# First mixture of experts by routed token rows instead of all experts over all tokens

## What is computed

```python
x = ln(x + L0_attn(x))    # 16 heads of 8, each token sees 7 neighbours
x = ln(x + L0_xattn(x))   # additive attention over 77 context tokens, tanh, two gates
x = ln(x + L0_ffn(x))     # first mixture, below
x = ln(x + L1_attn(x))    # keeps the 32 largest scores of each token
x = ln(x + L1_xattn(x))   # softmax attention over the context
x = ln(x + L1_ffn(x))     # second mixture: 8 experts (GELU, 256 hidden), one shared

def L0_ffn(x):            # 8 experts, 512 hidden, the best 2 of each token count
    probs = softmax(x @ gate_w.T); w, idx = top_k(probs, 2); w = w / w.sum()
    combine = zeros(T, 8).at[arange(T), idx].add(w)
    for gup, dn, ce in experts:
        g, u = split(x @ gup.T, 2)
        acc = acc + ce[:, None] * (silu(g) * u @ dn.T)
```

## Time and profile before

| | |
|---|---|
| Median of 2 runs | 874.55 us (874.15 to 874.95) |
| The profiled execution | 871.73 us, of it 869.9 us span |
| TensorE busy, share of the span | 736.0 us, 85% |
| VectorE, ScalarE, GpSimd busy | 505.5, 410.6, 77.0 us |
| Mean granted TensorE clock | 0.934 of full speed |
| First mixture's stage, batches 0 to 3 | 97.2, 96.8, 97.2, 76.1 us |

### The profile page before, as it was taken

The page is one execution under the profiler, slowest core; times in us unless marked ns, Lnnn a source line. Parts: engine busy times, 40 slices in busy tenths (PEclk is TensorE's granted clock), DMA queues, the critical chain, the costliest instruction groups (busy, mean ns, idle before and its releaser), DMA issues.

```text
span 869.9 us, 10866 instructions
## 1 busy us (share of the span) xinstructions
PE 736.0 (85%) x4056; PEld 511.7 (59%) x4056; DVE 505.5 (58%) x1420; ACT 410.6 (47%) x652; POOL 77.0 (9%) x71
## 2 busy tenths in 40 slices
PE   3468679999987999999978999999978999963596
PEld 1211157876244976775345967865347888843486
DVE  3678455654765675643845675733946754448344
ACT  1058643237875453247874443166964522211142
POOL 2100020100011120100011120100011000000100
PEclk8769879999999999999999999999999999986588
DMA  7025000000000010000000010000000000000000
GB/s 244 0 73 205 1 28 1 1 1 2 1 3 0 1 41 1 1 1 1 1 3 0 2 41 0 1 2 1 1 3 1 1 13 1 1 0 1 0 1 13
DMA packets 6549, 15.02 MB, mean 17 GB/s; under 512 B 2776, under 2 KB 2912, under 8 KB 6240
## 3 DMA queue, kind: packets, MB, share of 16 engines
q1 hardware_dynamic: 6496, 14.32, 4.9%
HBM read 13.27 MB, written 1.05 MB: 16 GB/s over the span
## 4 chain that ended last, share of the span: by engine, by line
PE 59%; DVE 17%; ACT 15%; issue 7%; POOL 1%; DMA 1%; SPq 1%; POOLq 0%; DVEq 0%; ACTq 0%
PE bank L642 12%; ACT a_big L846 9%; PE bank L503 7%; PE bank L504 7%; PE bank L505 7%; PE bank L760 6%; PE bank L601 6%; PE bank L695 2%; PE bank L675 2%; PE bank L517 1%; DVE a_big L1032 1%; DVE a_big L1377 1%; PE bank L552 1%; DVE top L1260 1%; DVE b_big L1264 1%
## 5 line engine op out<-in xcount | busy, mean ns | idle before, releaser
L877 ACT ACTIVATE b_big<-bank 128x512 f32<-128x512 f32 x128 | 75.2, 596 | 174.0 <-PE bank L505 173.8
L1228 DVE TENSOR_TENSOR b_big<-bank,b_big 128x512 f32<-128x512 f32 x128 | 87.8, 689 | 117.2 <-PE bank L505 66.8
L846 ACT ACTIVATE a_big<-a_sum,txt_cols 128x512 f32<-128x512 f32 x231 | 145.6, 715 | 14.2 <-PE bank L601 14.1
L601 PE MATMUL bank<-a_big,score_pad 128*32 128x512 f32 x616 | 143.9, 615 | 7.4 <-ACT a_big L966 5.8
L642 PEld LDWEIGHTS bank<-down_sb,b_big 128*128 128x128 f32 x1024 | 118.6, 192 | 6.5 <-issue 4.2
L642 PE MATMUL bank<-down_sb,b_big 128*128 128x128 f32 x1024 | 119.8, 275 | 0.5 <-DVE b_y L1217 0.5
L503 PE MATMUL bank<-x_hi,gup_hi 128*128 128x512 f32 x256 | 110.3, 431 | 5.2 <-ACT b_big L877 3.1
L504 PE MATMUL bank<-x_hi,gup_lo 128*128 128x512 f32 x256 | 101.8, 398 | 0.0
L505 PE MATMUL bank<-x_lo,gup_hi 128*128 128x512 f32 x256 | 101.8, 397 | 0.0
L601 PEld LDWEIGHTS bank<-a_big,score_pad 128*32 128x32 f32 x616 | 28.3, 109 | 101.3 <-ACT a_big L846 54.7
L760 PEld LDWEIGHTS bank<-rw_sb,b_big 128*128 128x128 f32 x576 | 71.6, 196 | 3.1
(11 more groups left out here) (216 smaller groups left out, 940.8 us busy)
## 6 DMA issues: line engine op xcount, KB each, us to landing
b_big<-gup SPq DMA_DIRECT2D x8, 512.0 KB, 7.1
down_sb<-down SPq DMA_DIRECT2D x1, 2048.0 KB, 8.5
rw_sb<-rw SPq DMA_DIRECT2D x1, 1152.0 KB, 10.8
a_T<-x_T SPq DMA_DIRECT2D x4, 256.0 KB, 2.5
a_tok<-x_tok SPq DMA_DIRECT2D x4, 256.0 KB, 2.9
b_big<-rw SPq DMA_DIRECT2D x2, 512.0 KB, 3.5
y<-b_tok SPq DMA_DIRECT2D x4, 256.0 KB, 2.0
const_sb<-const SPq DMA_DIRECT2D x1, 872.0 KB
```

The source lines that it names most:

```text
L601: last = mm(P[2][32 * j:32 * j + 32, :], score_pad[:, 31 - i:63 - i], ring[k % RING], start=(i == 0), stop=(KCOL * (i + 1) + j >= KEYS))
L846: act(ring[k % RING], a_sum[:, 0:S], ACT.Tanh, bias=txt_cols[:, c:c + 1])\
L877: act(th[n % 3], P[3 + 2 * (c % 2)][:, :], ACT.Silu).then_inc(th_ready, 1)
L1228: tt(hid[e % 2][:, c * S:(c + 1) * S], P[4 + 2 * (c % 2)][:, :], th[n % 3], ALU.mult)\
```

## The change

Only `swiglu` of every batch and what feeds it change. The tokens are no longer run through all experts. For each token the two best experts are found by rank (`rank_x2`, nine DVE instructions). `positions` on PE sums one-hot rows over earlier tokens, and `place_x2` (ten DVE instructions) turns that into a slot for each of the 1024 pairs of token and expert, sorted by expert, every expert beginning at a multiple of 128. That needs at most NT = 15 tiles of 128 rows. `scatter` on POOL writes the rows of x2 to their slots in device memory with 8 indirect DMAs of 128 rows of 512 bytes; `load_rows` on SP reads them back with 4 DMAs. For each tile PE loads the expert's offset into a register, transposes 128 rows, forms gate and up part in two halves of 256 hidden units with the tokens as stationary and the weights as moving operand (512 columns), transposes the product back in 4 pieces and does 4 down matmuls, whose weights are chosen by the register. The results go to device memory by 15 DMAs (`store_rows`), `gather` on POOL reads them back to token order with 8 indirect DMAs, and 8 DVE instructions weigh and add them. There are 30 steps of half a tile instead of 32; the steps of `attend_nearby` keep their numbers. A cleared x_rows and a separate load of the table `expand` come into the start of the program.

```diff
+NT = 2 * S // 128 + E - 1
+X_GROUPS = ((0, 1), (1, 3), (3, 7), (7, NT))
...
-SCORE_AT = (25, 28, 29, 31)
+SCORE_AT = (26, 28, 29)
...
+            def load_rows(b):
+                eng.wait_ge(scattered, 2 * T * 16 * (b + 1))
+                if b == 0:
+                    eng.wait_ge(split_done, len(raw))
+                else:
+                    eng.wait_ge(xout_psum, b)
+                for g, (i, z) in enumerate(X_GROUPS):
+                    eng.dma_start(rows_in[:, i * 128:z * 128].rearrange("p (i f) -> p i f", f=128),
+                                  x_rows[i * 128:z * 128, :].rearrange("(i p) f -> p i f", p=128))\
+                        .then_inc(rows_loaded[g], 16)
...
+            def store_rows(b):
+                if b >= 1:
+                    for t in range(T):
+                        eng.wait_ge(picked_in[t], 32 * b)
+                for i in range(NT):
+                    eng.wait_ge(y_ready, NT * b + i + 1)
+                    eng.dma_start(y_rows[i * 128:(i + 1) * 128, :], rows_out[i % 4]).then_inc(y_stored[i % 4], 16)
...
+            def positions(b):
+                eng.wait_ge(top_ready, b + 1)
+                at = P[2][:, 64:64 + (T + 1) * E]
+                mm(at, const_of("earlier"), r_top[:, :], start=True, stop=False)
+                for t in range(T):
+                    last = mm(at[:, (t + 1) * E:].rearrange("p (t e) -> p t e", e=E), ones[:, :],
+                              r_top[:, t * E:(t + 1) * E].unsqueeze(1).broadcast_to([128, T - t, E]),
+                              start=False, stop=(t == T - 1))
+                last.then_inc(pos_psum, 1)
...
+                def expert(i):
+                    at[i] = eng.value_load(offsets[0:1, i:i + 1], min_val=0, max_val=(E - 1) * I0)
...
+                def turn_x(i):
+                    for g, (first, end) in enumerate(X_GROUPS):
+                        if i == first:
+                            eng.wait_ge(rows_loaded[g], 16 * (b + 1))
+                    if i >= 1:
+                        eng.wait_ge(xT_lo_ready, NT * b + i)
+                    eng.transpose(tile(P[5], i % 2), tile(rows_in, i), ident).then_inc(xT_psum, 1)
+                def up(i, h):
+                    if h == 0:
+                        eng.wait_ge(xT_lo_ready, NT * b + i + 1)
+                    if i >= 1:
+                        eng.wait_ge(gated_ready, 2 * (NT * b + i - 1) + h + 1)
+                    half = slice(h * E * I0, (h + 1) * E * I0)
+                    hi = gup_hi[:, half][:, bass.ds(at[i], I0)]
+                    lo = gup_lo[:, half][:, bass.ds(at[i], I0)]
+                    mm(P[3 + h][:, :], xT_hi[i % 2], hi, start=True, stop=False)
+                    mm(P[3 + h][:, :], xT_hi[i % 2], lo, start=False, stop=False)
+                    mm(P[3 + h][:, :], xT_lo[i % 2], hi, start=False, stop=True).then_inc(gu_psum, 1)
+                def turn_h(i):
+                    eng.wait_ge(gated_ready, 2 * (NT * b + i + 1))
+                    if i >= 1:
+                        eng.wait_ge(hT_ready, NT * b + i)
                     for c in range(C0):
...
+                        last = eng.transpose(tile(P[6], c), tile(gated[i % 2], c), ident)
+                    last.then_inc(hT_psum, 1)
+                def down_mm(i):
+                    eng.wait_ge(hT_ready, NT * b + i + 1)
+                    if i >= 1:
+                        eng.wait_ge(y_ready, NT * b + i)
+                    for c in range(C0):
+                        w = down_sb[:, c * 128:][:, bass.ds(at[i], 128)]
+                        last = mm(tile(P[7], i % 4), tile(hid_T[i % 2], c), w, start=(c == 0), stop=(c == C0 - 1))
+                    last.then_inc(y_psum, 1)
+                expert(0)
+                turn_x(0)
+                for i in range(NT):
+                    if i + 1 < NT:
+                        expert(i + 1)
+                        turn_x(i + 1)
+                    for h in range(2):
+                        n = 2 * i + h
+                        up(i, h)
+                        if h == 0 and i >= 1:
+                            turn_h(i - 1)
+                        if h == 1 and i >= 2:
+                            down_mm(i - 2)
                         if ahead:
                             attend_nearby(b + 1, n, True)
                             if n in SCORE_AT:
                                 gate_scores(b + 1, SCORE_AT.index(n), SCORE_AT.index(n) + 1)
-                down_mm(E - 1)
+                turn_h(NT - 1)
+                down_mm(NT - 2)
+                down_mm(NT - 1)
...
+                def turned_x(i):
+                    eng.wait_ge(xT_psum, NT * b + i + 1)
+                    if i >= 2:
+                        eng.wait_ge(gu_psum, 2 * (NT * b + i - 1))
+                    act(xT_hi[i % 2], tile(P[5], i % 2), ACT.Copy).then_inc(xT_hi_ready, 1)
+                def turned_h(i):
+                    eng.wait_ge(hT_psum, NT * b + i + 1)
+                    if i >= 2:
+                        eng.wait_ge(y_psum, NT * b + i - 1)
+                    act(hid_T[i % 2], P[6][:, :], ACT.Copy).then_inc(hT_ready, 1)
+                turned_x(0)
+                for i in range(NT):
+                    if i + 1 < NT:
+                        turned_x(i + 1)
+                    for h in range(2):
+                        n = 2 * i + h
+                        eng.wait_ge(gu_psum, 2 * NT * b + n + 1)
+                        if i >= 2:
+                            eng.wait_ge(gated_ready, 2 * (NT * b + i - 2) + h + 1)
+                        act(silu_sb[i % 2][:, h * 256:(h + 1) * 256], P[3 + h][:, 0:256], ACT.Silu)\
+                            .then_inc(silu_ready, 1)
+                        if h == 0 and i >= 1:
+                            turned_h(i - 1)
                         if ahead:
                             attend_nearby(b + 1, n)
                             if n in GATE_AT:
                                 gate_tanh(b + 1, GATE_AT.index(n), GATE_AT.index(n) + 1)
+                turned_h(NT - 1)
...
+                eng.wait_ge(rank_step, n + 6)
+                ts(r_top[:, 0:T * E], r_rank[:, :], 2.0, None, ALU.is_lt).then_inc(top_ready, 1)
...
+            def place_x2(b):
+                n = PLACE_STEPS * b
+                pos = P[2][:, 64:64 + T * E].rearrange("p (t e) -> p t e", t=T)
+                count = P[2][:, 64 + T * E:64 + (T + 1) * E]
+                eng.wait_ge(pos_psum, b + 1)
+                tt(fills, count.unsqueeze(1).unsqueeze(3).broadcast_to([128, E, E, T]),
+                   const_of("fill").rearrange("p (e j m) -> p e j m", e=E, j=E), ALU.is_gt).then_inc(place_step, 1)
+                eng.wait_ge(place_step, n + 1)
+                red(d_prev[:, :], r_gt.rearrange("p (e n) -> p e n", e=E), AX, ALU.add).then_inc(place_step, 1)
...
+                eng.wait_ge(place_step, n + 6)
+                eng.tensor_copy(slots[:, :], slot_f[:, :]).then_inc(slots_ready, 1)
+                eng.wait_ge(place_step, n + 5)
+                ts(offsets[0:1, 0:NT], tile_e[0:1, 0:NT], float(I0), None, ALU.mult).then_inc(offsets_ready, 1)
...
+                def halves(i):
+                    eng.wait_ge(xT_hi_ready, NT * b + i + 1)
+                    tt(xT_lo[i % 2], tile(P[5], i % 2), xT_hi[i % 2].bitcast(F32), ALU.subtract).then_inc(xT_lo_ready, 1)
+                def take(i):
+                    eng.wait_ge(y_psum, NT * b + i + 1)
+                    if i >= 4:
+                        eng.wait_ge(y_stored[i % 4], 16 * (stores_of(i % 4) * b + i // 4))
+                    eng.tensor_copy(rows_out[i % 4], tile(P[7], i % 4)).then_inc(y_ready, 1)
...
+                halves(0)
+                for i in range(NT):
+                    if i + 1 < NT:
+                        halves(i + 1)
+                    for h in range(2):
+                        n = 2 * i + h
+                        eng.wait_ge(silu_ready, 2 * NT * b + n + 1)
+                        if i >= 2:
+                            eng.wait_ge(hT_psum, NT * b + i - 1)
+                        tt(gated[i % 2][:, h * 256:(h + 1) * 256], P[3 + h][:, 256:512],
+                           silu_sb[i % 2][:, h * 256:(h + 1) * 256], ALU.mult).then_inc(gated_ready, 1)
+                        if h == 1 and i >= 2:
+                            take(i - 2)
...
+                for t in range(T):
+                    eng.wait_ge(picked_in[t], 32 * (b + 1))
+                    stt(tile(b_y, t), picked[2 * t], r0_w[:, t:t + 1], tile(a_x2, t), ALU.mult, ALU.add)\
+                        .then_inc(mixed0, 1)
+                for t in range(T):
+                    eng.wait_ge(mixed0, 2 * T * b + t + 1)
+                    stt(tile(b_y, t), picked[2 * t + 1], r0_w[:, T + t:T + t + 1], tile(b_y, t), ALU.mult, ALU.add)\
+                        .then_inc(mixed0, 1)
+                norm_b(b, 1, mixed0, 2 * T * (b + 1))
...
+            def scatter(b):
+                eng.wait_ge(slots_ready, b + 1)
```

(20 more changed lines are left out.)

332 lines of the change are left out of this document (194 added, 138 removed).

## The result

938.4 us (median; 937.6 to 939.1) against 874.6: ratio 1.073, 95% interval 1.068 to 1.078, slower. The forecast was 948 (870 to 1020). The profiled execution has a span of 935.8 us, 65.9 more than before.

What follows compares the result with a forecast made beforehand. TensorE was taken to bound the kernel, above all in the first mixture. Terms -120 + 40 + 75 + 58 + 10 + 11 = +74 us on 871.7 gave 946, median 948 us, 8% slower; range 870 to 1020 us.

Steps and rivals of the forecast that it cites:

- registers: Register load and ten register instructions per tile on TensorE: 0.67 us a tile, +40 us in 60 tiles (0 to +120).
- crowding: Next batch's attention pieces beside the first mixture: stalls of 3 us in three batches, 1.5 at start, +11 us (0 to +30).
- TensorE's work: First mixture: fewer up and down matmuls, 75 transposes added, net 30.1 us a batch less, -120 us in four.
- passage in: Hole ahead of the first mixture (positions, scatters, read back): 19.6 us a batch; with extras and table loads, together +75 us.
- passage out, drain: Behind the first mixture: store, gathers, sums, plus 1.3 us of TensorE idle at the last tile: 14.9 us a batch, +58 us.
- clock: TensorE's lower clock level after a wait costs 1.6 us; seven more such places from the new holes: about +10 us.
- d: Price on POOL of each indirect DMA in scatters and gathers, taken as 1.1 us; each 0.1 us is 6.4 us.
- Faster: Rival: POOL only hands over indirect DMAs, d = 0.33, registers hidden: 848 us; decides below d = 0.47; chance 0.10.
- Registers bind: Rival: the register load is a round trip, 2.0 us a tile, and TensorE also loses clock: 1028 us; chance 0.12.
- serial DMAs: Rival: POOL holds each indirect DMA until its descriptors are taken, d = 2.4: 1031 us; chance 0.10.
- No change: Rival: d = 0.7 and the registers mostly hidden (+10): 885 us; chance 0.13.
- the first rival: The rival "Faster": 848 us with d = 0.33 and registers hidden; chance 0.10.

Runs made afterwards that it cites:

- e1_static: Against the changed kernel, each tile's weights are chosen by a constant, with the register load and its arithmetic removed: 934.1 us.
- e3_order: Against the changed kernel, the transposes of the previous tile's product and ScalarE's copy of them moved behind the second up product: 922.6 us.
- e8_plain: Against the changed kernel, the eight scatters and eight gathers of a batch became plain transfers to and from fixed places, issued by SP: 884.6 us.

## Why the prediction was right, term by term

The sign was right for the reason given: the journey through memory, the two passages, costs more than TensorE's saved work. That the size came out within 10 us of 948 is in part luck: two terms, registers and crowding, were wrong by 36 and 28 us, in opposite directions. With the first alone put right the forecast would have been 912, with the second alone 976. In us:

| term | forecast | measured |
|---|---|---|
| TensorE's work | -120 | -117: the last batch's mixture, 76.0 to 46.7, times four |
| registers | +40 | +4 (e1_static) |
| crowding | +11 | about +39: the other three mixtures shrank by 17.7, 15.4 and 15.4, not 29.3. 16 of it went with the order (e3_order) |
| passage in | +75 (+81 of holes, -6 of table loads) | +77: 19.2 in each of three batches (the 19.0 of the table and the 0.25 of before), 22.0 in batch 0; the second mixtures -2.5 in all, not explained |
| passage out, drain | +58 | +58: 14.8, 14.2, 14.1 and, in the last batch, 15.4 |
| clock | +10 | +8 in the middle stages; inside the mixtures it is part of the first and third rows |
| sum | +74 | +66 between the spans |

The registers' 4 lie for the most part inside the mixtures' 39; without them the column adds up to 65, and the spans differ by 66.

**Work and holes.** The step from one expert's chain to the tile's price held: 2.84 us measured, 2.9 forecast for free registers. The hole of 19.2 us matches 19.6 although d is 1.27 and not 1.1, since what stands beside the scatters was taken 1.8 us too long: the landing counts from the start of the last scatter, not from its end (0.7), and the read back of the first tile took 1.78 us and not 2.4 (0.6). The neighbour chosen for d, GpSimd's shortest instruction, came out near (1.0 there, 0.96 here), which is luck: nothing shows that a pow of four columns and an indirect DMA take their time for one reason. The 0.30 us between two issues was missing. The two ACT table loads that the forecast put into the hole are not there: at batch 1's they start at 326.55 and 349.93 us, before it and behind it. The passage out's equal figures are partly luck too: by this measure the drain of 1.3 us a batch lies inside the mixture, and without it the forecast was 53.

**Registers: a step that failed.** It read "nearest to the row of the same sequencer", 0.06 us a record from logits of 8 columns. Those rows are of eight short matmuls of 8 columns. In the mixture the array has work for all of a tile's 2.84 us, and the forecast's 0.67 us of issue work, if it is that much, has cover there. The sentence that "most of a tile is already issue-bound" is not borne out: without the register instructions a tile took 2.85 us.

**Crowding: the other.** Three us a batch were worked out for tanh on ScalarE. The waits were of another kind: the product on VectorE behind the next batch's pieces, with TensorE standing at `turn_h` (7.4 of 11.5 us in batch 1). Beside them stands a lower clock. By windows over the mixtures of batches 0 to 2, TensorE had no work for 3.5, 4.5 and 4.9 us before and for 11.3, 11.5 and 11.2 us after, while in the last batch this fell from 2.1 to 0.8; an estimate from these numbers is that 25 of the 39 us are idle time. The other 14 came with a lower granted clock: 0.98, 1.00 and 1.00 before, 0.92, 0.89 and 0.88 after. What in the mixtures brings the clock down stays open, and so do the 23 us that e3_order left. The forecast counted busy time against step time (1.3 us of DVE in 2.9), which says nothing of how late a product may be: the slack was one half's three matmuls, 0.7 us, and VectorE's pieces of the next batch stand ahead of the product in its queue.

**Clock.** The forecast's 1.6 us behind each hole has a counterpart. The two matmuls with k1 and q1 before and after, from the chains:

```profile
412.64 1.13 PE bank L670 x2
413.77 0.87 PE bank L671 x2
```

```profile
451.48 2.07 PE bank L807 x2
453.55 1.72 PE bank L808 x2
```

3.79 in place of 2.00 us, at a granted clock of 0.78 in the first 10 us behind the hole and 1.00 before; with the transposes ahead of them 2.3 us. The forecast counted 1.6 us for all seven places. Those ahead of the mixtures are in other rows of the table: the last batch's mixture ran at 0.94, which over 46.7 us is 2.8 us, an estimate, and makes its fall of 29.3 us smaller than what the matmuls alone would give.

**Rivals.** Faster: refuted, and by e8_plain even close to its own condition. Registers bind, serial DMAs: refuted (2.84 us a tile; 1.27 from start to start). No change asked for d = 0.7 and registers mostly hidden, which they were; with 0.57 us less for each of 64 indirect DMAs it would still be 902 us, as an estimate. Landings of 2.0 to 2.5 us "however many bytes", on which the first rival leaned, are those of 40 to 256 KB; in the same trace 512 KB took 7.1 us.

**The signs.** Holes of about 20 us on both sides of the mixture with eight DMAs each: seen (19.0 and 20.7 us in batch 1). TensorE's busy time was to fall by 100 us or more and fell by 70: a matmul at the lower clock is busy for longer, and the mean granted clock of the execution fell from 0.93 to 0.84. A tile was to take 3.6 us and the last batch's mixture 54; they took 2.84 and 46.7, the sign that the forecast itself named for free registers.

## What to carry to other kernels

Work taken from the bound engine is worth its full price only where nothing else sets its pace: ask of every handover how late the other engine may be, not how busy it is. A trip through memory costs its issues one by one and its landing once, so put the issues beside work (per tile, on the idle engine) and leave only the last one for the end; here that was shown for the way out alone. What fills a hole becomes the bound once the hole is shortened; test the fillers again after each cut.

## What was new about the hardware

An indirect DMA of 128 rows of 512 bytes held GpSimd for 0.96 us plus 0.30 to the next, whether it scattered or gathered, and landed 2.2 to 2.5 us after it started; SP issued plain ones of the same size 0.46 us apart on average (8 in 3.67), and they landed in 1.6 us. The granted clock inside mixtures with short waits was 0.88 to 0.94, and 374 matmuls took from 65.1 to 70.5 us with it; between mixtures of the same code and the same idle time it differed by up to 0.04. Register loads and register-addressed weights on TensorE did not lengthen a tile of 2.84 us.
